# Moving steps of the opening, of the end of self attention and of the output path in a decoder layer

## The chip, the core and the metric

The kernel runs on one core of a Trainium2 chip. The metric is the device time in microseconds (us) of one execution. The engines are named as in the profile: PE is TensorE (PEld its weight loads), DVE is VectorE, ACT is ScalarE, POOL is GpSimd, SP is the sync engine that issues transfers.

## What is computed

One decoder layer over 8 batches of 512 tokens of 256 features, in float32. The reference, cut to its stages:

```python
x = layernorm(x + self_attn(x))            # 16 heads, gated linear attention with level factors and decays
x = layernorm(x + cross_attn(x, ctx_1024)) # 16 heads of 16, 1024 keys, softmax, output projection
x = layernorm(x + ffn(x))                  # 32 experts, each takes its top 8 tokens

# in self_attn
dt  = softplus(x @ Wdt.T + dt_bias); g = -exp(A_log) * dt
Lam = softplus(Lp * (x @ Wdl.T))
decay = exp(cumsum(g)[t] - cumsum(g)[s])
W = (Q K^T) * S ** -0.5 * decay * Lam[level(t, s)]
y = (W V) @ Wout.T + x
```

## The kernel before

**Order of stages.** `self_attention`, `cross_attention` and `experts_and_combine` run one after the other, each in a block of its own: the next begins when all engines have finished the one before. Every engine has its own program with waits on semaphores. In the two attentions the work goes through sections `first` (batch 0), `mid` (batches 1 to 6), `last` (batch 7) and `tail`. In a section, `now` is the batch in work, `prev` the batch before, whose last pieces are still to be done, and `nxt` the batch behind, which is being prepared.

**Opening of self attention** (`sec == "pro"`). DVE evaluates log1p as a polynomial twice: over the level factors `lam` (`log1p_poly`, nine instructions of 640 columns, L93 and L96) and over the time steps `dt_g` (nine of 512 columns). For the latter `decay_sums` first adds a bias to PE's result, writes a tile of ones and forms -|z|, and waits for ACT's exponential of it (L761). A scan gives `cg` (`cg_ready`). PE transposes `cg`, POOL forms distances from it, ACT exponentiates them, and PE and ACT turn them into `dec` (`dec_ready`). `spread_sums` hands the sums to POOL's `differences` (L856), ACT takes their absolute value and exponential (L785, L787), and DVE multiplies the result into `NEAR` (L1046). `level_factors` (L1027 to L1031) and `block_factors` (L1001, L1005) stand behind `spread_sums`.

**End of self attention** (`sec == "tail"`, i = 0 to 7, of which PE has 4). PE finishes the last two head pairs, transposes y (L465), projects it (L673), and also prepares batch 0 of cross attention: `cross_tokens` (transposes of x, L575), `cross_queries` (L585), `cross_keys` (L601) and `cross_values` (L593). `sa_jobs` and `CROSS_JOBS` list the same jobs in the same order for the PSUM slots. DVE splits queries and keys into three bf16 parts (`parts`, L186 to L195), and does the layer norm between.

**Cross attention.** A batch has 32 steps: 4 quads of heads by 8 chunks of 128 keys. In each step PE makes the scores of four heads (L1489), which ACT exponentiates (L1625), multiplies the step before by the values (L1450), and makes four tiles of scores for the maxima 12 steps ahead (L1428), which DVE reduces (L1716); these tiles have three PSUM slots, used in turn. Every eighth step PE also transposes the maxima (L1437) and DVE copies them out (L1737). The other work of a batch is tied to steps: PE transposes the next batch's x in step 0, projects half of its own values in step 1 (L1415), the next batch's queries in step `PROJECT_Q` = 4 (L1406) and its keys in steps 7 and 12 (L1398), transposes the previous batch's normalised x in step 9 (L1561), and projects the values' other half in step 20.

**Outputs.** When a quad of heads is done, `take_outputs` transposes its sum out of PSUM (L1744). `outputs` then takes a reciprocal (L1750), multiplies (L1752) and transposes again (L1756), and SP copies the result into `oT` (`move_o`, L1281). For quads 2 and 3 of the previous batch both calls stand in step 1. In step `PROJECT_O` = 4, PE waits for the copies (`o_moved`) and projects the outputs (L1507), DVE adds x and forms mean and variance (L1782 to L1791, `var`), and in step `NORM` = 7 normalises (L1795). Quad 0 of the batch in work is scaled and transposed in step `GATE_MAX` = 12, just ahead of the gate's MAX8.

**POOL in cross attention** does its work in this order, whatever the steps are; the splitting of queries and keys takes four pieces of four operations each:

```python
if prev:
    pool.wait_ge(var, b)
    nc.gpsimd.tensor_tensor(rstd[:, :, 0], mv[:, :, 1], sh.mhalf[:, 0:G], ALU.pow).then_inc(rstd_ready, 1)
if nxt:
    ...
    parts(ca, pool, nc.gpsimd, 2, b * 3 + 4, pieces=4)
```

`parts` first waits until ACT has copied the projection into the one buffer `R`; ACT in its turn (`evac_whole`) copies the next projection only when the parts of the one before have been made:

```python
src = full(name)
act.wait_ge(parts_ready, (b + 1) * 3 + (n + 1) % 3)
nc.scalar.copy(R[:], src).then_inc(act_evac, 1)
```

Scores and projections share two PSUM slots (`psA`), in the fixed order that `ca_jobs` lists, and ACT's queue is in order too.

Of the kernel before, what the change touches and what calls it, by code (L numbers as in the profile page):

```python
# [88 lines left out]

def log1p_poly(eng, acc, u):  # L90

    c = _log1p_coefficients()
    eng.tensor_scalar(acc, u, c[0], None, ALU.mult)  # L93
    eng.drain()
    for ck in c[1:]:
        eng.scalar_tensor_tensor(out=acc, in0=acc, scalar=ck, in1=u, op0=ALU.add, op1=ALU.mult)  # L96
        eng.drain()
# [39 lines left out]
STACKED = 16 * 2 * len(Q_PARTS)  # L137
X1T, PROJECT_V1, PROJECT_Q, PROJECT_O, NORM = 0, 1, 4, 4, 7
PROJECT_K, X2T, COPY_X2, GATE, GATE_MAX, GATE_EXP, TOP8, TOP8_T, PICK, PICK_T = (7, 12), 9, 10, 10, 12, 14, 20, 21, 28, 29
PROJECT_V0, LAST_OUTPUTS = 20, 27  # L140
BEHIND_JOBS = (PROJECT_V1 + 1, PROJECT_K[0] + 1)
# [133 lines left out]

CROSS_JOBS = {0: ["cq"], 2: [("ck", 0)], 3: [("ck", 1), "cv"]}


def sa_jobs(section):

    now, prev, nxt = flags(section)
    a, v = [], []
    if section == "pro":
        return ["dl", ("v", 0)], v
    for i in range(PAIRS if now else 4):
        a += [("state", i)] * (sa_pair(section, i, 2) is not None)
        a += ["x1T"] * (i == 0 and section == "tail")
        a += [("qk", i)] * now
        a += ["yT"] * (i == 2 and prev)
        a += [("ktok", i)] * (sa_pair(section, i, 1) is not None)  # L290
        a += ["dl"] * (i == 0 and nxt) + [("v", 1)] * (i == 2 and now) + [("v", 0)] * (i == 5 and nxt)
        a += CROSS_JOBS.get(i, []) if section == "tail" else []
        v += [("score", i)] * (sa_pair(section, i, 1) is not None)
        v += [("far", i)] * (sa_pair(section, i, 2) is not None)
        v += [("out", 0), ("out", 1)] * (i == 3 and prev)
    return a, v
# [4 lines left out]
SA_DVE = Lane({s: sa_jobs(s)[1] for s in SECTIONS}, DVE_SLOTS)  # L301
SCALE = S ** -0.5
ZERO = len(_log1p_coefficients())
POOL_POLY = {2: (0, 2)}
# [11 lines left out]
def self_attention(nc, sh, dram):  # L316
    with ExitStack() as ctx:
# [103 lines left out]
        def _(pe):  # L421
            def body(sec, b):
# [194 lines left out]
                for i in range(PAIRS if now else 4):  # L617
                    one, two = sa_pair(sec, i, 1), sa_pair(sec, i, 2)
                    if two is not None:
                        states(i, two)  # L620
                    if sec == "tail" and i == 0:
                        cross_tokens()
                    opening = sec == "first" and i == 1
# [52 lines left out]
                    if sec == "tail":  # L676
                        if i == 0:
                            cross_queries()
                        if i == 2:
                            pe.wait_ge(ca.ctx_loaded, 16)  # L680
                            cross_keys(0)
                        if i == 3:
                            cross_keys(1)
                            pe.wait_ge(ca.wv_loaded, 16)
                            cross_values()
# [5 lines left out]
        def _(act):  # L691
            def body(sec, b):
# [71 lines left out]
                for i in range(PAIRS):  # L764
                    steps = i < (PAIRS if now else 4)
                    if steps and sa_pair(sec, i, 2) is not None:
                        nc.scalar.copy(Mst[:, 1:16, :], full(("state", i))[:, HD:16 * HD].rearrange("q (s c) -> q s c", c=HD)
                                       ).then_inc(act_evac, 1)
                    if sec == "tail" and i == 0:
                        nc.scalar.copy(ca.x1T[:].rearrange("p k t -> p (k t)"), full("x1T")).then_inc(act_evac, 1)  # L770
                    if now:
# [28 lines left out]
                    if i == 6 and nxt:  # L800
                        decays()
                    if sec == "tail" and i == 0:
                        cross_whole("cq", 0)
                    if sec == "tail" and i == 6:
# [173 lines left out]
        def _(dve):  # L978
# [3 lines left out]
            def body(sec, b):  # L982
# [81 lines left out]

                def decay_sums():

                    dve.wait_ge(dt_full, 1)
                    nc.vector.tensor_scalar(dt_z, bank(0), dtb[:, 0:1], None, ALU.add)
                    nc.vector.memset(ones, 1.0)
                    dve.drain()  # L1070
                    negated_abs(nc, dt_g, dt_z).then_inc(dt_abs, 1)
                    dve.wait_ge(dt_exp, 1)
                    log1p_poly(nc.vector, dt_g, dt_u)

                    nc.vector.scalar_tensor_tensor(out=dt_g, in0=dt_z, scalar=0.0, in1=dt_g, op0=ALU.max, op1=ALU.add)
                    dve.wait_ge(rate_ready, 1)
                    dve.drain()
                    nc.vector.tensor_scalar(dt_g, dt_g, alog[:, 0:1], -1.0, ALU.mult, ALU.mult)
                    dve.drain()
                    nc.vector.tensor_tensor_scan(out=cg, data0=ones, data1=dt_g, initial=0.0, op0=ALU.mult, op1=ALU.add  # L1080
                                                 ).then_inc(cg_ready, 1)

                if sec == "pro":
                    nc.vector.memset(ca.zero[:], 0.0)
                    dve.wait_ge(level_loaded, 16 * 3)
                    dve.wait_ge(expz, 1)
                    log1p_poly(nc.vector, lam[:].rearrange("p g h l -> p (g h l)"), ul[:])
                    dve.wait_ge(dt_loaded, 16 * 3)
                    decay_sums()
                    dve.wait_ge(cgt_ready, 1)  # L1090
                    spread_sums()
                    level_factors()
                    block_factors()
                    dve.wait_ge(zeroed, 3)
                    dve.wait_ge(dec_ready, 1)
                    return
# [129 lines left out]
def cross_attention(nc, sh, dram):  # L1226
    with ExitStack() as ctx:
# [467 lines left out]
        def _(dve):  # L1695
# [8 lines left out]
            def body(sec, b):  # L1704
# [25 lines left out]
                def max_rows(pos):  # L1730
                    for name in max_step(pos)[1]:
# [7 lines left out]
                        dve.nop().then_inc(dve_evac, 1)  # L1739

                def take_outputs(bb, q):

                    dve.wait_ge(av_done, (bb * QUADS + q + 1) * KT)
                    nc.vector.transpose(byq[q % 2][:].rearrange("p c s -> p (c s)"), acc[:]).then_inc(acc_evac, 1)  # L1744
                    dve.drain()

                def outputs(bb, q):

# [4 lines left out]
                                            ALU.mult)  # L1753
                    dve.drain()
                    dve.wait_ge(o_moved[q % 2], bb * 32 + (q // 2 + 1) * 16)
                    nc.vector.transpose(byd[q % 2][:], t[:].rearrange("p c s -> p (c s)")).then_inc(o_ready, 1)  # L1756
# [9 lines left out]
                for s in range(STEPS if now else TAIL_STEPS):  # L1766
                    maxima = now and (nxt or s + LEAD < STEPS)
                    if maxima:
                        max_jobs(s + LEAD, 0, 1)
                    if prev and s == 1:  # L1770
                        if sec != "tail":
                            outputs(b - 1, 2)
                        outputs(b - 1, 3)
                    if prev:
# [31 lines left out]
                        if s == GATE_MAX:  # L1806
                            if sec == "mid":
                                dve.wait_ge(l_moved, b * (16 * G))
                            if now:
                                outputs(b, 0)  # L1810
                            nc.vector.max(m8[:], L[:])
# [19 lines left out]
                        if s == PICK_T:  # L1831
                            nc.vector.tensor_copy(sh.mT[:, :, :, bass.ds(b - 1, 1)].rearrange("p k e o -> p k (e o)"),
                                                  full("mT")[:, 0:KD * P].rearrange("p (k e) -> p k e", k=KD)[:, :, 0:E]
                                                  ).then_inc(dve_evac, 1)
                    if sec == "first" and s == GATE_MAX:
                        outputs(b, 0)
                    if now and s == TOP8:
# [379 lines left out]
```

## Time and profile before

| what | us |
|---|---|
| median of 3 runs (range) | 1792.65 (1788.92 to 1797.26) |
| the profiled execution, time | 1791.35 |
| its span, first to last instruction | 1789.6 |
| opening, until the steady part of self attention | 0 to 61 |
| self attention, batches | 61 to 580 |
| its end | 580 to 629 |
| cross attention, batches 0 to 7 | 661 to 1605 |
| its tail | 1605 to 1632 |
| experts and combination | 1632 to 1790 |

Busy shares over the whole span are PE 93%, DVE 71%, ACT 46% and POOL 33%. They are averages over stages with different limits; a row of the timeline tells when one instruction (or several alike, one after the other) started, how long it took, and in brackets how long its engine had been idle and what ended that.

### The profile page before, as it was taken

Reading aid. Unit: us, or ns where it says so; the run is one execution under the profiler, and the core shown is the slowest. Engines: PE = TensorE matmul, PEld = TensorE weight load, DVE = VectorE, ACT = ScalarE, POOL = GpSimd, SP = SyncE. Lnnn points to the kernel's source line nnn. Section 1 sums busy time; section 2 is a strip of 40 time slices with the busy share of each in tenths; the row PEclk is TensorE's granted clock in tenths of the full one; section 3 lists DMA queues with packets and bytes.
Section 4 is the critical chain, followed back from the end, with each engine's and each line's share of the span. In section 5 each row is a group of like instructions: output and inputs, shape, how many; then the busy total and the mean of one; then the engine's idle time right before and its main releaser. Section 6 shows DMA issues by size and latency. Waiting matters only on the chain. (4 is left out here: it accounts for less than half of the span.)

```text
span 1789.6 us, 48945 instructions
## 1 busy us (share of the span) xinstructions
PE 1659.9 (93%) x19942; PEld 802.0 (45%) x19942; DVE 1277.5 (71%) x2414; ACT 814.5 (46%) x981; POOL 587.1 (33%) x926
## 2 busy tenths in 40 slices
PE   6899999999999789999999999999999999898557
PEld 3566666666666423343343333433433434234224
DVE  5667677677774577888878889788788888842004
ACT  2334343343342215656556656565466565561103
POOL 3535545554552454316034043060250420000002
PEclk8999999999999859999999999999999999998879
DMA  7000000000000130211111202211112121438995
GB/s 258 3 4 3 3 3 3 3 3 3 3 33 3 36 93 25 86 57 44 59 57 48 92 32 78 67 44 59 57 44 81 36 74 60 192 116 344 420 419 217
DMA packets 66062, 146.04 MB, mean 82 GB/s; under 512 B 12320, under 2 KB 36128, under 8 KB 58176
## 3 DMA queue, kind: packets, MB, share of 16 engines
q1 hardware_dynamic: 65296, 142.34, 21.9%
q8 instruction: 157, 2.57, 0.6%
q10 hardware_dynamic: 560, 0.72, 0.2%
q14 instruction: 49, 0.40, 0.1%
HBM read 92.43 MB, written 7.86 MB: 56 GB/s over the span
## 5 line engine op out<-in xcount | busy, mean ns | idle before, releaser
L1716 DVE TENSOR_REDUCE mx<-cpsV 128x1 f32<-128x512 f32 x1024 | 652.9, 685 | 114.2 <-PE cpsV L1428 93.7
L1625 ACT ACTIVATE w<-cpsA 128x1024 f32<-128x1024 f32 x512 | 496.3, 1021 | 253.6 <-PE cpsA L1489 248.5
L1428 PE MATMUL cpsV<-w 96*128 96x512 bf16 x1024 | 332.5, 394 | 29.0 <-DVE mx L1716 16.1
L1489 PE MATMUL cpsA<-w 99*128 99x512 bf16 x1024 | 272.3, 381 | 5.8 <-ACT w L1603 3.4
L1450 PE MATMUL cacc<-w 128*32 128x512 f32 x2048 | 273.3, 606 | 0.4 <-ACT w L1625 0.4
L472 PE MATMUL psA<-w 128*128 128x512 f32 x512 | 257.9, 627 | 8.3 <-DVE WT L1105 3.5
L1428 PEld LDWEIGHTS cpsV<-w 96*128 96x128 bf16 x1024 | 85.3, 98 | 308.8 <-DVE mx L1716 227.5
L1683 POOL TENSOR_TENSOR crstd<-cmv,mhalf 128x4 f32<-128x4 f32 x8 | 8.2, 1019 | 579.9 <-DVE cmv L1791 579.9
L772 ACT COPY w<-psA 128x1024 f32<-128x1024 f32 x64 | 64.8, 1013 | 233.4 <-PE psA L472 233.4
L1489 PEld LDWEIGHTS cpsA<-w 99*128 99x128 bf16 x1024 | 93.8, 97 | 135.3 <-ACT w L1625 10.9
L890 POOL TENSOR_TENSOR VP<-V,VPF 128x128 f32<-128x128 f32 (+2 forms) x256 | 130.1, 540 | 44.4 <-PE psA L485 39.8
L1114 DVE TENSOR_TENSOR tmp<-psV,CF 128x512 f32<-128x512 f32 x64 | 44.3, 692 | 112.4 <-PE psV L535 111.9
L472 PEld LDWEIGHTS psA<-w 128*128 128x128 f32 x512 | 88.4, 192 | 79.8 <-issue 69.3
L186 POOL TENSOR_TENSOR w<-w,zero 128x256 bf16<-128x256 f32 x88 | 51.2, 613 | 122.1 <-ACTq L1604 122.1
L1450 PEld LDWEIGHTS cacc<-w 128*32 128x32 f32 x2048 | 41.0, 108 | 94.0 <-issue 89.8
L2114 DVE TENSOR_TENSOR z<-psE,b1T 128x256 f32<-128x256 f32 x8 | 3.4, 425 | 110.7 <-PE psE L2044 110.7
L2058 PE MATMUL psE<-w,hT 128*32 128x256 f32 x512 | 37.6, 458 | 38.7 <-DMA w<-in_w 36.8
L1121 DVE TENSOR_REDUCE w<-tmp 128x128 f32<-128x512 f32 x64 | 67.6, 1056 | 4.7
L1603 ACT COPY w<-cpsA 128x1024 f32<-128x1024 f32 x21 | 21.3, 1013 | 96.5 <-PE cpsA L1398 49.7
L505 PEld LDWEIGHTS psV<-w 64*32 64x32 f32 x4096 | 41.2, 106 | 48.9 <-issue 47.7
L1415 PEld LDWEIGHTS cpsA<-w,w 128*128 128x128 f32 x480 | 54.7, 192 | 12.6 <-ACT w L1625 12.6
L195 POOL TENSOR_TENSOR w<-w 128x256 bf16<-128x256 f32 x88 | 57.2, 679 | 3.1
(232 smaller groups left out, 2202.3 us busy)
## 6 DMA issues: line engine op xcount, KB each, us to landing
w<-in_w SPq DMA_DIRECT2D x56, 1024.0 KB, 16.4
w<-w SPq DMA_DIRECT2D x189, 128.0 KB, 2.3
w<-w SPq DMA_DIRECT2D x189, 64.0 KB, 2.0
w<-in_ctxT SPq DMA_DIRECT2D x8, 1024.0 KB, 5.2
w<-in_xT SPq DMA_DIRECT2D x8, 512.0 KB, 6.4
x_tok<-in_x SPq DMA_DIRECT2D x8, 512.0 KB, 9.7
w<-in_w SPq DMA_DIRECT2D x8, 512.0 KB, 17.2
out_y<-w SPq DMA_DIRECT2D x16, 256.0 KB, 2.3
```

The costliest lines, as they stand in the source:

```text
L186: ops.tensor_tensor(cut(high, m), cut(r, m), zeros, ALU.add)
L195: ops.tensor_tensor(cut(low, m), cut(r, m), cut(mid, m), ALU.subtract)
L472: last = nc.tensor.matmul(out[:, n * T:(n + 1) * T], w[:, k, i * P:(i + 1) * P], XT[:, b, k, :], start=(k == 0), stop=(k == KD - 1))
L772: nc.scalar.copy(QK[:, i % 4, :], full(("qk", i))).then_inc(act_evac, 1)
L890: last = nc.gpsimd.tensor_tensor(VP[:, p % 2, g, 0:n, :].rearrange("q n (h c) -> q n h c", c=HD), vv.unsqueeze(1).broadcast_to([P, n, 2, HD]),
L1121: nc.vector.tensor_reduce(yp, tmp[:].rearrange("p g s c -> p g c s"), AX_X, ALU.add)
L1415: last = nc.tensor.matmul(out[:, c * P:(c + 1) * P], cT[:, k, c * P:(c + 1) * P], wv[:, k, hv * P:(hv + 1) * P], start=(k == 0), stop=(k = ...
L1428: nc.tensor.matmul(out, Qst[q // 2][0:ROWS, hh, g * P:(g + 1) * P], Kst[q // 2][0:ROWS, hh, half * BANK:(half + 1) * BANK], start=True, st ...
L1450: last = nc.tensor.matmul(acc[BLK * jj:BLK * (jj + 1), :], Vc[:, chunk, 4 * q + jj, :], Pr[:, (2 * s + jj // 2) % 4, (jj % 2) * T:(jj % 2 ...
L1489: last = nc.tensor.matmul(out[:, n * T:(n + 1) * T], Kst[q // 2][0:ROWS + 3, hh, chunk * P:(chunk + 1) * P], Qst[q // 2][0:ROWS + 3, hh, : ...
L1625: nc.scalar.activation(Pr[:, (2 * s + pp) % 4, :], src, ACT.Exp, scale=CA_SCALE).then_inc(act_evac, 1)
L1716: nc.vector.tensor_reduce(mx[:, q % 2, row, k % 2:k % 2 + 1], full(m[k]), AX_X, ALU.max).then_inc(dve_evac, 1)
```

## The change

Four things are moved; no arithmetic is added or dropped.

1. Opening: seven of the nine polynomial instructions over `lam` come first, then bias, ones and -|z| of the time steps, then the last two, then `level_factors`, then the polynomial over the time steps and the scan. `level_factors` stood behind `spread_sums`.
2. End of self attention: the transposes of x stand at the end of i = 0 and no longer near its start, the queries in i = 1 and not 0, the first half of the keys in i = 3, behind the output projection, and not in i = 2.
3. Cross attention, quad 0: reciprocal and multiplication are in step 9, the transposition stays in step 12.
4. Cross attention, quad 3 of the previous batch: `outputs` stands in step 4 and not 1 (but in `tail` in step 1, as before), and the output projection with its additions and statistics in step 5 and not 4.

```diff
-def log1p_poly(eng, acc, u):
+def log1p_poly(eng, acc, u, first=0, last=None):
...
-X1T, PROJECT_V1, PROJECT_Q, PROJECT_O, NORM = 0, 1, 4, 4, 7
+X1T, PROJECT_V1, PROJECT_Q, PROJECT_O, NORM = 0, 1, 4, 5, 7
...
-PROJECT_V0, LAST_OUTPUTS = 20, 27
+PROJECT_V0, LAST_OUTPUTS, SCALE_OUTPUTS = 20, 27, 9
...
-CROSS_JOBS = {0: ["cq"], 2: [("ck", 0)], 3: [("ck", 1), "cv"]}
+CROSS_JOBS = {0: ["x1T"], 1: ["cq"], 3: [("ck", 0), ("ck", 1), "cv"]}
...
-                    if sec == "tail" and i == 0:
-                        cross_tokens()
...
                     if sec == "tail":
                         if i == 0:
+                            cross_tokens()
+                        if i == 1:
                             cross_queries()
-                        if i == 2:
+                        if i == 3:
                             pe.wait_ge(ca.ctx_loaded, 16)
                             cross_keys(0)
-                        if i == 3:
                             cross_keys(1)
...
-                    log1p_poly(nc.vector, lam[:].rearrange("p g h l -> p (g h l)"), ul[:])
+                    lamf = lam[:].rearrange("p g h l -> p (g h l)")
+                    log1p_poly(nc.vector, lamf, ul[:], 0, BEFORE_STEPS)
                     dve.wait_ge(dt_loaded, 16 * 3)
+                    time_steps()
+                    log1p_poly(nc.vector, lamf, ul[:], BEFORE_STEPS)
+                    level_factors()
                     decay_sums()
                     dve.wait_ge(cgt_ready, 1)
                     spread_sums()
-                    level_factors()
                     block_factors()
...
-                    if prev and s == 1:
-                        if sec != "tail":
-                            outputs(b - 1, 2)
+                    if prev and s == 1 and sec != "tail":
+                        outputs(b - 1, 2)
+                    if prev and s == (1 if sec == "tail" else PROJECT_O - 1):
                         outputs(b - 1, 3)
...
                             if now:
-                                outputs(b, 0)
+                                turn_outputs(b, 0)
...
+                    if now and s == SCALE_OUTPUTS:
+                        scale_outputs(b, 0)
                     if sec == "first" and s == GATE_MAX:
-                        outputs(b, 0)
+                        turn_outputs(b, 0)
```

`scale_outputs` is the first half of `outputs` (reciprocal and multiplication, each with a drain), `turn_outputs` the second (the wait for the buffer and the transposition); `time_steps` is the first part of `decay_sums` up to -|z|.

## Rows read from the trace of the kernel before

**Rows 1.** windows, batch 2: length, busy PE PEld DVE ACT POOL, clock, DMA share
```profile
894.67:1015.70 121.03, 118.41 (x670) 45.37 (x669) 102.89 (x195) 69.79 (x75) 35.61 (x57) 1.00 0.18 59
```

**Rows 2.** timeline, TensorE, batch 2: start, length, line, operands, count
```profile
912.60 3.69 PE L1507 MATMUL cpsV<-cwo,oT 128*128 128x256 f32 x16
...
917.22 3.70 PE L1406 MATMUL cpsA<-w 128*128 128x512 f32 x8
...
923.07 1.07 PE L1450 MATMUL cacc<-w 128*32 128x512 f32 x8
...
924.51 0.81 PE L1489 MATMUL cpsA<-w 99*128 99x512 bf16 x3
...
929.73 3.70 PE L1398 MATMUL cpsA<-w,w 128*128 128x512 f32 x8
```

**Rows 3.** timeline, VectorE, batch 2, steps 1 and 4; idle before in brackets
```profile
903.36 0.26 DVE L1750 RECIPROCAL rec<-byq 128x16 f32<-128x16 f32 x1
...
904.19 0.71 DVE L1756 STREAM_TRANSPOSE byd<-byq 128x512 f32<-128x512 f32 x1
...
914.72 0.69 DVE L1782 TENSOR_TENSOR o<-cpsV,x_tok 128x512 f32<-128x512 f32 x1
...
918.51 0.17 DVE L1791 TENSOR_SCALAR cmv<-cmv 128x4 f32<-128x4 f32 x1
```

**Rows 4.** timeline, GpSimd, batch 2, steps 4 to 7
```profile
918.76 1.03 POOL L1683 TENSOR_TENSOR crstd<-cmv,mhalf 128x4 f32<-128x4 f32 x1 [69.66 <-DVE cmv L1791]
...
922.16 2.33 POOL L186 TENSOR_TENSOR w<-w,zero 128x256 bf16<-128x256 f32 x4 [2.37 <-ACTq L1604]
...
929.80 2.70 POOL L195 TENSOR_TENSOR w<-w 128x256 bf16<-128x256 f32 x4
```

**Rows 5.** timeline, ScalarE, batch 2, step 7
```profile
933.54 1.01 ACT L1603 COPY w<-cpsA 128x1024 f32<-128x1024 f32 x1 [3.55 <-PE cpsA L1398]
```

**Rows 6.** source view of L1281, the copies of outputs
```profile
DMA to landing us min/median/max: 2.6/2.6/6.3
```

**Rows 7.** timeline, batch 2, steps 9 and 13
```profile
940.63 2.62 DVE L1716 TENSOR_REDUCE mx<-cpsV 128x1 f32<-128x512 f32 x4 [0.93 <-PE cpsV L1428]
...
954.75 0.10 PEld L1428 LDWEIGHTS cpsV<-w 96*128 96x128 bf16 x1 [0.60 <-DVE mx L1716]
```

**Rows 8.** timeline, TensorE, batch 7, steps 4 and 13
```profile
1516.00 3.69 PE L1507 MATMUL cpsV<-cwo,oT 128*128 128x256 f32 x16
...
1553.52 0.39 PE L1428 MATMUL cpsV<-w 96*128 96x512 bf16 x1 [2.69 <-DVE mx L1716]
```

**Rows 9.** windows around gaps of TensorE; columns as in group 1
```profile
44.80:47.30 2.50, 0.00 (x0) 0.00 (x0) 2.27 (x7) 2.50 (x3) 2.36 (x9) 1.00 0.01 3
...
50.70:54.20 3.50, 0.04 (x3) 0.01 (x1) 3.28 (x5) 0.65 (x2) 1.82 (x2) 0.80 0.00 0
...
54.20:59.60 5.40, 5.40 (x47) 2.82 (x48) 1.67 (x8) 1.01 (x1) 3.63 (x3) 0.50 0.01 2
...
1554.70:1558.10 3.40, 3.40 (x13) 0.73 (x6) 2.28 (x4) 0.04 (x1) 0.00 (x0) 0.50 0.12 42
```

**Rows 10.** timeline, end of self attention
```profile
603.18 4.88 PE L601 MATMUL psA<-w,w 128*128 128x512 f32 x8
...
607.90 3.62 PE L673 MATMUL psV<-wo,w 128*128 128x256 f32 x16
...
618.58 1.23 DVE L195 TENSOR_TENSOR w<-w 128x1024 bf16<-128x1024 f32 x1
```

**Rows 11.** timeline, opening
```profile
25.03 0.43 DVE L93 TENSOR_SCALAR w<-w 128x512 f32<-128x512 f32 x1 [0.69 <-ACT w L761]
...
47.76 1.91 ACT L787 ACTIVATE w<-w 128x2048 f32<-128x2048 f32 x1
...
51.05 1.27 DVE L1046 TENSOR_TENSOR w<-w,w 128x1024 f32<-128x1024 f32 x1
```

**Rows 12.** source view of L1031: count, ns min/median/max, first and last start
```profile
L1031 DVE TENSOR_SCALAR w<-w,tconst x40: 266/274/1087, 40.7 to 510.3; 128x64 f32<-128x64 f32 x40
```

More of the change, by code:

```diff
@@ L87, in negated_abs @@
     return nc.vector.scalar_tensor_tensor(out=out, in0=x, scalar=-1.0, in1=x, op0=ALU.mult, op1=ALU.min)
-def log1p_poly(eng, acc, u):
+def log1p_poly(eng, acc, u, first=0, last=None):
     c = _log1p_coefficients()
-    eng.tensor_scalar(acc, u, c[0], None, ALU.mult)
-    eng.drain()
-    for ck in c[1:]:
+    if first == 0:
+        eng.tensor_scalar(acc, u, c[0], None, ALU.mult)
+        eng.drain()
+    for ck in c[max(first, 1):last]:
         eng.scalar_tensor_tensor(out=acc, in0=acc, scalar=ck, in1=u, op0=ALU.add, op1=ALU.mult)
@@ L286, in sa_jobs @@
         a += [("state", i)] * (sa_pair(section, i, 2) is not None)
-        a += ["x1T"] * (i == 0 and section == "tail")
         a += [("qk", i)] * now
@@ L302 @@
 SCALE = S ** -0.5
+BEFORE_STEPS = 7
 ZERO = len(_log1p_coefficients())
@@ L768, in body @@
                                        ).then_inc(act_evac, 1)
-                    if sec == "tail" and i == 0:
-                        nc.scalar.copy(ca.x1T[:].rearrange("p k t -> p (k t)"), full("x1T")).then_inc(act_evac, 1)
                     if now:
@@ L802, in body @@
                     if sec == "tail" and i == 0:
+                        nc.scalar.copy(ca.x1T[:].rearrange("p k t -> p (k t)"), full("x1T")).then_inc(act_evac, 1)
+                    if sec == "tail" and i == 1:
                         cross_whole("cq", 0)
@@ L1063, in output_factors, with time_steps @@
                     dve.drain().then_inc(lam_used, 1)
-                def decay_sums():
+                def time_steps():
                     dve.wait_ge(dt_full, 1)
@@ L1071, in decay_sums @@
                     negated_abs(nc, dt_g, dt_z).then_inc(dt_abs, 1)
+                def decay_sums():
                     dve.wait_ge(dt_exp, 1)
@@ L1739, in max_rows, with outputs @@
                         dve.nop().then_inc(dve_evac, 1)
+                def outputs(bb, q):
+                    scale_outputs(bb, q)
+                    turn_outputs(bb, q)
                 def take_outputs(bb, q):
@@ L1745, in take_outputs, with scale_outputs @@
                     dve.drain()
-                def outputs(bb, q):
+                def scale_outputs(bb, q):
                     t = byq[q % 2]
@@ L1754, in outputs, with turn_outputs @@
                     dve.drain()
+                def turn_outputs(bb, q):
+                    t = byq[q % 2]
                     dve.wait_ge(o_moved[q % 2], bb * 32 + (q // 2 + 1) * 16)
```

## Prediction

> **What bounds the kernel now.** I read the page, then the busy times by windows, then the timeline stage by stage. In the windows the reader is to see that a batch of cross attention takes 121.03 us, of which PE is busy 118.41, at full granted clock [rows 1]. There are six such batches (1 to 6), each within 0.9 us of this length. So PE is the bound, DVE (102.89) stands close behind, and POOL (35.61) seems far off. That last share misleads: in the timeline POOL's work lies in bursts that ACT, and through ACT PE, must wait for. What is moved is therefore judged by order and due time, not by busy time.
>
> In the timeline of batch 2 the steps 4 to 8 read so: PE projects the outputs from 912.60 to 916.29, then the queries from 917.22 to 920.92, begins step 6 at 924.51 and the first half of the keys at 929.73 [rows 2]. DVE gives the variance at 918.68 [rows 3], POOL has its power done at 919.79, then idles 2.37 us until ACT has copied the queries, and splits them from 922.16 to 932.50: 10.34 us [rows 4]. ACT copies the keys at 933.54, and by its row it waited for PE's projection [rows 5]. POOL's split was done only 1.04 us before. That margin is what the change spends.
>
> **Output projection in step 5 (batches 1 to 6).** Steps 4 and 5 first. The projection's 3.69 us leave step 4 and enter step 5; the queries come 3.66 earlier. DVE now scales quad 3 where it began the additions, at 914.72; from the reciprocal to the end of the transposition that takes 903.36 to 904.90 = 1.54 [rows 3], so the copy is issued at about 916.35 and lands 2.6 us later [rows 6], near 919.0. Everything of step 5 up to its values, which stood at 923.07 [rows 2], comes 3.66 earlier too (the queries used to follow at once on the projection, 917.22 against 913.56 now), and the projection takes the place of the values: 923.07 − 3.66 = 919.4. The copy is in time by 0.4 us, the projection ends at E = 923.1, and step 6 begins 1.4 later (923.07 to 924.51 is 1.44 [rows 2]), where it began before. The step's PE work is neutral. Bounds: 0, and 3.7 if the copy takes its longest, 6.3.
>
> Now what hangs on it. From the projection's end (916.29) to the variance (918.68) are 2.39 us, to the end of the power 3.50 [rows 3, 4]. The query projection used to lie in those 3.5 us, so POOL waited for ACT. Now ACT has copied the queries at 922.1 − 3.7 = 918.4, but POOL, in order, waits for `var`: it starts the split at E + 3.6 and ends at E + 3.6 + 10.34 = E + 13.95 = 937.05. ACT can have PE's keys at E + 1.4 + (933.54 − 924.51) = E + 10.4 = 933.5; about 0.5 of DVE's statistics also come between PE and its next tile in step 6, which this wait swallows. ACT may copy only when the split is done, so it stands 3.5 us, with the exponentials of step 8 behind it; PE makes two scores and two tiles and stands too, since the next scores need the slot that ACT has not emptied. DVE has nothing to reduce. I find nothing that hides it: 3.5 us in each of six batches = **+21.0**. The next projection (step 12) comes 19 us later, and POOL's second split takes 10.2: no further wait. SP's later copy also holds back the context's transfer, which the queue has behind it: from 905.7 to about 917; with a median landing of 5 us it is there by 922, needed at 930. The maxima's copy behind that is needed in step 8 too. Both nothing.
>
> **Clock.** PE would stand from about 935.3 (two tiles after step 8's first scores) to 938.1, 2.8 us. After a gap of 3.5 us the clock was granted at 0.50 for the next 5.4 us; after the gap of 2.69 in batch 7 it was 0.50 for 3.40 us; after one of 2.5 us it stayed at 1.00 in that stretch [rows 8, 9]. In a low stretch of 3.40 us PE does what takes 1.7 at the full level. I take 1.7 in five of the six batches: **+8.5**; bounds 0 (no drop) and 6 × 3.4 = 20.4 (a stretch of 6.8). The Trainium skill (TensorE: Matmul & The Clock Gate, "HAM oscillation — how this bites in real kernels") says that a wait which returns in each tile can put the clock down each time, half of the low time being lost; by it the term would be 6 × 1.7 = 10.2 and the forecast 1.7 higher. The row at 44.8 is why I count five.
>
> **Quad 0 scaled in step 9.** Reciprocal and multiplication are 0.83 us (903.36 to 904.19 [rows 3]). In step 9 DVE idles 0.93 us while PE transposes x [rows 7]: covered, in batches 1 to 7. What they leave is step 12, whose overrun PE meets in step 13: a wait of 0.60 at 954.75 [rows 7] and one of 0.5 behind it, of which step 13's excess over batch 0 is 0.65. I take 0.65 × 6 = **−3.9**, bounds 0 and 6 × 0.83. In batch 7 PE waits 2.69 there [rows 8] with nothing to cover: −0.8. Batch 0 has no transposition of x in step 9: +0.3.
>
> **Batch 7.** It projects no queries, so step 4 has only 2.83 us of PE work against DVE's maxima, row factors and now the scaling. DVE's copy is ready 3.75 after where the projection began (912.60 to 916.35), so at 1516.00 + 3.75 + 2.6 + 0.1 = 1522.45 landed; PE could project one step later than before, at 1518.85 [rows 8]. The wait is 3.6, of which 0.5 is now spent on DVE anyway: **+3.1**, with step 13 +2.3. Bounds 0 and 3.6. The tail keeps its scaling in step 1 and has no steps' work between; nothing changes. Weights for the experts follow the end of this stage, so a shift here reaches the end.
>
> **End of self attention.** Before, the keys' half (4.88 us from 603.18) stood ahead of the output projection at 607.90, and everything behind ran through DVE: additions, statistics and the split of the keys until 619.81 [rows 10], then ACT for another 8.8. Now y is done ahead of the queries. PE's sum from the last head pair is queries (3.6 to 5.4, by clock) + transposes 1.4 + ACT's copy 1.1, now uncovered, + projection 3.62 + keys 3.6 to 4.88, which with 1.0 for ACT's copy and 5.1 for the split puts the split's end at 614.4 to 617.9. Against 619.81: −5.4 to −1.9; I take **−3.8**.
>
> **Opening.** ACT's exponential, for which DVE idled 0.69 [rows 11], is now behind two polynomial instructions. `level_factors` comes in ahead of `cg`: its five L1031 take 0.27 each when POOL is quiet and up to 1.09 beside POOL [rows 12]; with the two others 2.2 us. `cg` comes 1.5 later, and all of POOL, ACT and PE that follows it. DVE has 5 us less behind it, but `NEAR` at 51.05 waits for ACT's exponential, done at 49.67 [rows 11], which moves by the same 1.5; only DVE's last doubling between (1.4) falls away. Net **+0.2**, bounds 0 and +1.5.
>
> **Sum.** 21.0 + 8.5 − 3.9 + 0.3 + 2.3 − 3.8 + 0.2 = +24.6. On the profiled execution's 1791.35 us that is 1816. The median of the runs is 1.3 above the profiled time; I leave that inside the range.
>
> **Rivals.**
> - *The wait, but the clock holds* (chance 0.20). For it: the row at 44.8, and PE works until 2.8 us before the copy. Then 1791.35 + 16.1 = 1807.5.
> - *Longer low stretches* (0.12): 6.8 us each, as seen from 52.8 to 59.6 in the opening; 1791.35 + 16.1 + 20.4 = 1828.
> - *The split of the queries ends in time* (0.06), the other side. It decides at 10.4 − 3.6 = 6.8 us for the split, or if `var` came 3.5 us earlier. Against it: all its operations of 2.3 to 2.7 us for four are steady rows. Then only −3.9, +0.3, +2.3, −3.8, +0.2 stay: 1786.5, not slower.
> - *Nothing shows* (0.04): each gain and loss is eaten by slack elsewhere, 1791 to 1796.
>
> My forecast has 0.58. Range: the forecast's own runs from 1809 to 1823 by the ends of the self-attention and batch 7 terms; to hold 8 in 10 it must take in the first rival, and with the copy's late landings part of the second: 1802 to 1829. A change under 0.5% (9 us) can hardly be told from none here: faster 0.03, same 0.09, slower 0.88.
>
> **What would show it.** Step by step in the profile after: in batches 1 to 6 ACT's copy of the keys (L1603, step 7) ended by POOL, some 3.5 us after PE's projection, and the same batches near 125 to 126 us instead of 121.0; the granted clock below 1.00 in them; no wait of PE for DVE in step 13; DVE idle in step 1; the first cross-attention instruction about 4 us earlier than 628.9; batch 7 about 2 us longer. It is wrong if the copy L1603 still follows PE directly, for then the largest term is gone, or if PE waits for `oT` in step 5 by more than 0.5 us.

## The result and the profile after

| | before | after |
|---|---|---|
| median of the runs (range), us | 1792.65 (1788.92 to 1797.26) | 1824.69 (1819.52 to 1826.51) |
| profiled execution: time, span | 1791.35, 1789.6 | 1819.52, 1817.8 |

The changed kernel is slower: the ratio is 1.0168, with a 95% interval of 1.0139 to 1.0196. The profiled execution is the shortest of the three of after; the other two took 5.2 and 7.0 us more, at a mean granted clock of 0.954 and 0.953 against 0.959. Of the 28.2 us between the two profiled spans, the part up to cross attention's first reduction gives back 8.0, batch 0 takes 1.6, batches 1 to 6 take 27.8, batch 7 takes 6.1 and the stages behind it 0.7.

The windows of after, one for each batch shown (columns as in [rows 1]), then one low stretch of the clock in batch 1:

```profile
768.06:893.74 125.68, 121.04 (x670) 46.55 (x669) 102.73 (x195) 69.79 (x74) 35.74 (x57) 0.97 0.17 57
893.74:1018.71 124.97, 119.68 (x670) 45.74 (x669) 103.01 (x195) 69.79 (x74) 35.73 (x57) 0.99 0.17 57
...
1144.92:1272.65 127.73, 122.47 (x670) 46.50 (x669) 102.60 (x195) 69.89 (x75) 35.70 (x57) 0.96 0.17 56
...
1397.83:1521.32 123.49, 118.14 (x669) 45.34 (x668) 102.76 (x195) 69.79 (x75) 30.62 (x49) 1.00 0.18 58
1521.32:1627.30 105.98, 98.93 (x531) 33.05 (x529) 72.36 (x145) 63.85 (x69) 1.02 (x1) 0.94 0.35 138
811.90:818.70 6.80, 6.80 (x26) 2.54 (x23) 3.88 (x7) 2.78 (x4) 6.38 (x11) 0.50 0.00 0
```

Two losses are to be seen. Batch 6 ran at full granted clock and with no more busy time of PE than [rows 1], and still took 123.49 (120.88 before): this is waiting. The others took 1.5 to 4.2 us more than batch 6, the more the lower their mean clock: 0.99, 0.97, 0.96.

The wait stands in the timeline of after, batch 1, steps 4 to 8, rows of all engines in order of time:

```profile
786.14 3.70 PE L1412 MATMUL cpsA<-w 128*128 128x512 f32 x8
...
788.10 0.71 DVE L1771 STREAM_TRANSPOSE byd<-byq 128x512 f32<-128x512 f32 x1
...
788.84 0.51 SPq L1287 DMA_DIRECT2D oT<-byd  x1
...
789.96 1.01 ACT L1609 COPY w<-cpsA 128x1024 f32<-128x1024 f32 x1 [3.56 <-PE cpsA L1412]
...
791.91 3.62 PE L1513 MATMUL cpsV<-cwo,oT 128*128 128x256 f32 x16
...
797.73 0.17 DVE L1806 TENSOR_SCALAR cmv<-cmv 128x4 f32<-128x4 f32 x1
...
797.98 1.02 POOL L1689 TENSOR_TENSOR crstd<-cmv,mhalf 128x4 f32<-128x4 f32 x1 [73.57 <-DVE cmv L1806]
...
798.97 2.33 POOL L187 TENSOR_TENSOR w<-w,zero 128x256 bf16<-128x256 f32 x4
...
802.74 3.70 PE L1404 MATMUL cpsA<-w,w 128*128 128x512 f32 x8
...
806.76 2.55 POOL L196 TENSOR_TENSOR w<-w 128x256 bf16<-128x256 f32 x4
...
809.39 1.01 ACT L1609 COPY w<-cpsA 128x1024 f32<-128x1024 f32 x1 [6.39 <-POOLq L197]
...
810.46 0.61 PE L1495 MATMUL cpsA<-w 99*128 99x512 bf16 x2 [2.63 <-ACT w L1609]
```

ACT had copied the queries at 790.97, but POOL split them only from 798.97, because it stood at the power (L1689), which needs the variance of 797.90. In [rows 4] the order was the same, but the power was over before the queries had been copied. The split ends at 809.31; ACT's copy of the keys, in [rows 5] released by PE, is now released by POOL, and PE waits 2.63 us for the slot that ACT has not emptied. The page's costliest groups say it for the whole kernel (busy, mean ns, idle before, and how much of it the named releaser ended):

```profile
L1495 PE MATMUL cpsA<-w 99*128 99x512 bf16 x1024 | 278.0, 387 | 21.3 <-ACT w L1609 19.1
...
L1609 ACT COPY w<-cpsA 128x1024 f32<-128x1024 f32 x21 | 21.3, 1012 | 91.6 <-POOLq L197 38.3
```

38.3 is six times 6.39, one wait in each of the batches 1 to 6. The 6.80 us at granted clock 0.50 begin 1.4 us after PE's wait has ended, with PE at work in between.

The timeline of TensorE after, in the opening, the end of self attention, batch 7, and the end of the kernel:

```profile
54.22 1.98 PE L473 MATMUL psA<-w 128*128 128x512 f32 x4 [1.71 <-DVE WT L1111]
...
592.01 3.70 PE L586 MATMUL psA<-w 128*128 128x512 f32 x8
...
598.03 3.69 PE L672 MATMUL psV<-wo,w 128*128 128x256 f32 x16 [1.45 <-ACT w L772]
...
1541.83 0.39 PE L1434 MATMUL cpsV<-w 96*128 96x512 bf16 x1 [1.06 <-DVE mx L1722]
...
1543.66 6.42 PE L1513 MATMUL cpsV<-cwo,oT 128*128 128x256 f32 x16 [0.64 <-DMA oT<-byd]
...
1803.15 1.99 PE L2016 MATMUL psE<-x_tok,ident 128*128 128x256 f32 x8 [3.11 <-ACT w L2119]
```

### The profile page after: what moved, and what is told of

Read it like the earlier page. It is cut to its first block and busy times, and to the rows that moved or that the text cites. A ratio compares the mean times of both kernels' runs of the same rounds, so it can differ in the third digit from the quotient of the medians.

```text
span 1817.8 us, 48945 instructions
## 1 busy us (share of the span) xinstructions
PE 1667.3 (92%) x19942; PEld 802.7 (44%) x19942; DVE 1275.6 (70%) x2414; ACT 814.7 (45%) x981; POOL 586.8 (32%) x926
## 5 line engine op out<-in xcount | busy, mean ns | idle before, releaser
L1434 PE MATMUL cpsV<-w 96*128 96x512 bf16 x1024 | 337.0, 399 | 28.7 <-DVE mx L1722 18.5
L1495 PE MATMUL cpsA<-w 99*128 99x512 bf16 x1024 | 278.0, 387 | 21.3 <-ACT w L1609 19.1
L1456 PE MATMUL cacc<-w 128*32 128x512 f32 x2048 | 277.9, 615 | 0.4 <-ACT w L1631 0.4
L1689 POOL TENSOR_TENSOR crstd<-cmv,mhalf 128x4 f32<-128x4 f32 x8 | 8.1, 1018 | 622.0 <-DVE cmv L1806 622.0
L1495 PEld LDWEIGHTS cpsA<-w 99*128 99x128 bf16 x1024 | 95.0, 99 | 155.3 <-ACT w L1609 27.8
L187 POOL TENSOR_TENSOR w<-w,zero 128x256 bf16<-128x256 f32 x88 | 51.2, 614 | 114.6 <-ACTq L1610 114.6
L1609 ACT COPY w<-cpsA 128x1024 f32<-128x1024 f32 x21 | 21.3, 1012 | 91.6 <-POOLq L197 38.3
L1421 PEld LDWEIGHTS cpsA<-w,w 128*128 128x128 f32 x480 | 54.7, 192 | 12.6 <-ACT w L1631 12.6
```

Of the source, the lines that this page charges most:

```text
L1421: last = nc.tensor.matmul(out[:, c * P:(c + 1) * P], cT[:, k, c * P:(c + 1) * P], wv[:, k, hv * P:(hv + 1) * P], start=(k == 0), stop=(k = ...
L1434: nc.tensor.matmul(out, Qst[q // 2][0:ROWS, hh, g * P:(g + 1) * P], Kst[q // 2][0:ROWS, hh, half * BANK:(half + 1) * BANK], start=True, st ...
L1456: last = nc.tensor.matmul(acc[BLK * jj:BLK * (jj + 1), :], Vc[:, chunk, 4 * q + jj, :], Pr[:, (2 * s + jj // 2) % 4, (jj % 2) * T:(jj % 2 ...
L1495: last = nc.tensor.matmul(out[:, n * T:(n + 1) * T], Kst[q // 2][0:ROWS + 3, hh, chunk * P:(chunk + 1) * P], Qst[q // 2][0:ROWS + 3, hh, : ...
```

## The experiments

Each ratio is to the kernel before in the same session (medians 1790.7 to 1791.8), with its 95% interval. Lengths of batches are those of the one profiled execution, measured from the first exponential of one batch to that of the next, batch 7's to its last step.

**Part 4 undone, parts 1 to 3 kept.**

```diff
-X1T, PROJECT_V1, PROJECT_Q, PROJECT_O, NORM = 0, 1, 4, 5, 7
+X1T, PROJECT_V1, PROJECT_Q, PROJECT_O, NORM = 0, 1, 4, 4, 7
-                    if prev and s == 1 and sec != "tail":
-                        outputs(b - 1, 2)
-                    if prev and s == (1 if sec == "tail" else PROJECT_O - 1):
-                        outputs(b - 1, 3)
+                    if prev and s == 1:
+                        if sec != "tail":
+                            outputs(b - 1, 2)
+                        outputs(b - 1, 3)
```

> The changed kernel with quad 3's scaling back in step 1 and the output projection back in step 4; opening, end of self attention and the scaling of quad 0 stay changed. Theory (the order of GpSimd's queue: the variance comes late, so the split of the queries ends late, so ScalarE's copy of the keys and with it TensorE waits in step 8): batches 1 to 6 return to about 120.3 us (121.0 less 0.7 for step 13), batch 7 to about 99, the whole about 1780, that is 40 below the changed kernel and 11 below the kernel before. Rival (what stands in steps 9 and 12, or the opening, costs something in the batches): batches 1 to 6 stay above 121.

Measured: 1784.13 us, ratio 0.9957 (0.9944 to 0.9971). Batches 1 to 6 have full clock and 120.2 to 120.4 us each but for the first (119.54). The window of batch 2:

```profile
886.70:1007.08 120.38, 118.06 (x670) 45.39 (x669) 103.08 (x195) 69.81 (x74) 35.75 (x57) 1.00 0.18 59
```

Against the 121.03 of [rows 1] that is 0.65 us less, all of it in step 13 (2.93 us for 3.59): the quad scaled in step 9. Everything that made the change slow is in part 4. The batches came out as expected, the whole 4 us above the 1780 that was expected.

**Part 4 kept, GpSimd's order turned round.** The query split now stands ahead of the wait for the variance.

```diff
-                if prev:
-                    pool.wait_ge(var, b)
-                    nc.gpsimd.tensor_tensor(rstd[:, :, 0], mv[:, :, 1], sh.mhalf[:, 0:G], ALU.pow).then_inc(rstd_ready, 1)
                 if nxt:
...
                     parts(ca, pool, nc.gpsimd, 2, b * 3 + 4, pieces=4)
+                if prev:
+                    pool.wait_ge(var, b)
+                    nc.gpsimd.tensor_tensor(rstd[:, :, 0], mv[:, :, 1], sh.mhalf[:, 0:G], ALU.pow).then_inc(rstd_ready, 1)
```

> The changed kernel, and in GpSimd's queue the split of the queries is put ahead of the wait for the variance; output projection stays in step 5. Theory (GpSimd's order): no wait of TensorE for ScalarE's copy in step 8, no low clock there, batches 1 to 6 at about 120.8 us (123.5 in batch 6 of the changed kernel less 2.8), the whole about 31 below the changed kernel, near 1789. Rival (the projection in step 5 has lost the cover that the query projection gave, and that by itself is the loss): batches stay near 124, at most 1 us less each.

Measured: 1790.95 us, ratio 1.0005 (0.9992 to 1.0017). The timeline of its batch 2, then the windows of batches 2 and 7:

```profile
910.35 1.01 ACT L1609 COPY w<-cpsA 128x1024 f32<-128x1024 f32 x1 [3.55 <-PE cpsA L1412]
...
911.48 2.32 POOL L187 TENSOR_TENSOR w<-w,zero 128x256 bf16<-128x256 f32 x4 [68.78 <-ACTq L1610]
...
921.84 1.03 POOL L1693 TENSOR_TENSOR crstd<-cmv,mhalf 128x4 f32<-128x4 f32 x1 [0.18 <-issue]
...
927.03 1.01 ACT L1609 COPY w<-cpsA 128x1024 f32<-128x1024 f32 x1 [3.55 <-PE cpsA L1404]
```

```profile
887.64:1008.52 120.88, 118.04 (x670) 45.43 (x669) 101.57 (x195) 69.79 (x75) 35.59 (x57) 1.00 0.18 59
1491.78:1598.11 106.33, 99.25 (x531) 32.52 (x529) 72.41 (x145) 63.84 (x68) 1.02 (x1) 0.94 0.35 138
```

POOL splits at once, the keys' copy is released by PE again, and both the waits and the low clock are gone from batches 1 to 6. So not the moved projection as such, but the order of two things in POOL's queue made each of the six batches 4.8 us longer (753.3 us for the six in after, 724.2 here). What is left of the moved steps is 0.5 us a batch: 120.7 to 120.9 for the 120.2 to 120.4 with part 4 undone. Batch 7 stays at 106.

**Part 4 alone, on the kernel before** (the first diff, the other way round).

> The kernel before with the fourth part alone: quad 3 scaled in step 4, projection in step 5. Theory: all of the loss is in this part, so this is the slowest kernel: batches 1 to 6 at 124.2 us without a low clock and 125 to 129 with, batch 7 longer by 6, in sum 1791 + 19 + 12 + 6 = about 1828, some 9 above the changed kernel. Rival (the parts act together, the other three are neutral): about 1820, as the changed kernel.

Measured: 1820.39 us, ratio 1.0158 (1.0140 to 1.0176). Batches 1 to 6 took 123.4, 125.78, 127.14, 125.83, 125.58 and 124.09, the first and the last of them at full clock:

```profile
1402.25:1526.34 124.09, 118.48 (x669) 45.29 (x668) 102.56 (x195) 69.81 (x74) 30.40 (x49) 1.00 0.17 57
```

124.09 − 120.88 = 3.2 us of wait without the scaling's gain, near the predicted 3.5. The expected 1828 was missed; the time is the rival's 1820, and the other three parts gain nothing here that the runs can tell (after has 1.0168). In the two traces they do gain, 7.1 us ahead of batch 0 and 0.65 in each batch, but the clock takes much of it back: the low stretches of batches 1 to 6 add up to 30.6 us in after and to 17.1 in this trace.

**The wait filled.** In batches 1 to 6, ahead of step 8's first scores, PE makes 20 transposes of the identity into the slot that the scores then overwrite.

```diff
                             out = take_a(("s", s, pp))
+                            if s == 8 and pp == 0 and sec == "mid":
+                                for _ in range(20):
+                                    nc.tensor.transpose(out[:, 0:P], sh.ident[:], sh.ident[:])
```

> The changed kernel with 20 transposes of the identity (about 2.3 us of TensorE, results overwritten) ahead of the first scores of step 8 in batches 1 to 6, where TensorE would stand for 2.6 us anyway. Theory (part of the loss is the clock, which falls after the wait): the wait stays, the clock stays at full level, batches 1 to 6 all near 123.6 us, in sum 12 below the changed kernel's profiled 1819.5, about 1808. Rival (the low clock is hidden behind ScalarE and VectorE): as the changed kernel, or slower by the added work.

Measured: 1810.84 us, ratio 1.0102 (1.0082 to 1.0122), 0.66% or 12 us under the ratio of after, although nothing useful was added. The window of its batch 2, and in TensorE's timeline the fill and the wait that is left:

```profile
895.27:1018.91 123.64, 120.30 (x690) 47.65 (x689) 102.97 (x195) 69.81 (x75) 35.75 (x57) 1.00 0.18 58
```

```profile
934.77 2.35 PE L1495 MATMUL cpsA<-ident 128*128 128x128 f32 x20
936.96 0.60 PE L1498 MATMUL cpsA<-w 99*128 99x512 bf16 x2
...
938.54 0.61 PE L1498 MATMUL cpsA<-w 99*128 99x512 bf16 x2 [0.55 <-ACT w L1612]
```

ACT's copy still waits for POOL (6.41 us in this run), the batches take 123.4 to 123.6 (the first 122.77), like batch 6 of after, and no clock below 1.00 is granted in any of them. The six sum to 740.5 against 753.3 in after: 12.8 us for the clock. Against the 721.1 of part 4 undone the wait is the rest: 19.4 us, 3.2 a batch.

**The projection in step 5 in batch 7 alone, on the kernel before.** Quad 3 is turned in step 4 and the outputs projected in step 5 only where `sec == "last"`.

```diff
+def project_o(sec):
+    return 5 if sec == "last" else PROJECT_O
...
-                        outputs(b - 1, 3)
+                        if sec != "last":
+                            outputs(b - 1, 3)
+                    if sec == "last" and s == 4:
+                        outputs(b - 1, 3)
```

> The kernel before with one edit: in the last section alone, quad 3 of batch 6 is turned in step 4 and the output projection stands in step 5. The prediction priced this at 3.1 us (a wait of PE for the copied outputs). Theory by the trace of after: steps 4 and 5 together take 15.5 us where they took 10.4, a wait of about 3.5 with the clock then low, so batch 7 gets 4 to 6 us longer (99.8 before) and the time is 1794.5 to 1797. Rival one (the prediction's price, no clock): 3 us, 1793.5 to 1794.5. Rival two (slack later in the section takes it up): no change, 1790 to 1792.

Measured: 1797.46 us, ratio 1.0028 (1.0012 to 1.0045); some 5 us. TensorE's timeline of its batch 7:

```profile
1517.35 0.39 PE L1433 MATMUL cpsV<-w 96*128 96x512 bf16 x1 [1.06 <-DVE mx L1721]
...
1519.18 6.45 PE L1512 MATMUL cpsV<-cwo,oT 128*128 128x256 f32 x16 [0.62 <-DMA oT<-byd]
...
1556.02 1.21 PE L1433 MATMUL cpsV<-w 96*128 96x512 bf16 x2 [2.70 <-DVE mx L1721]
```

The projection took 6.45 where it took 3.69 [rows 8], 2.76 by the clock. Steps 4 to 6 are 5.6 us longer than in before: PE stood 2.8 us in them for 0.7, and was busy 16.1 for 12.6, in a low stretch of 6.8 us from 1517.9 on. Of the standing only 0.62 is for the copied outputs; the larger part is for DVE's maxima, behind the moved scaling and transposition. Steps 13 and 14 took another 2.6 in this execution, with a low stretch from 1555.5, within the wait of 2.70, to 1565.7; that wait is as long in before [rows 8]. Rival two (no change) falls by the interval. Rival one (a wait of 3 us and no clock) doesn't, since 3 us lie within it, but it falls by the trace, where the clock is low.

**Batch 7 put back, GpSimd's order turned, on the kernel after.** The second diff, and the projection in step 4 where `sec == "last"`.

> The kernel after with two edits: GpSimd splits the queries ahead of its wait for the variance, and in the last section alone quad 3 of the batch before is turned in step 1 and the output projection stands in step 4, as in the kernel before. The run with the first edit alone took 1790.95 us, and its batch 7 lasted 106.3 us to step 31, against 98.9 where the whole output path was put back. Theory (batch 7 has no query projection to cover the later copy, so the moved step costs it 5 to 7 us): batches 1 to 6 stay at 120.7 to 121.0, batch 7 lasts 99 to 102, and the time is 1784 to 1787. Rival (batch 7's excess was a low stretch of the clock that fell there by chance): batch 7 stays at 104 to 107 or lengthens elsewhere by the same, and the time is 1790 to 1792.

Measured: 1787.79 us, ratio 0.9974 (0.9957 to 0.9990). Batch 7:

```profile
1495.40:1594.08 98.68, 93.90 (x531) 30.81 (x529) 72.53 (x145) 63.85 (x68) 1.02 (x1) 0.98 0.38 148
```

98.68 for 106.33; the time is 0.8 above the theory's bound. The rival is half right: 4.6 of these 7.7 us lie in steps 4 to 6, which the edit puts back, and 3.1 in steps 13 and 14, where this execution had 3.4 us of low clock and the other 10.2. Even without the wait and without batch 7 the step brings nothing over leaving it undone: batches 1 to 6 took 120.8 to 121.2 but for the first, 0.5 to 0.8 more than with part 4 undone. Where these go is not shown.

**The opening alone, and the end of self attention alone, each on the kernel before** (parts 1 and 2 of the change).

> The kernel before with the new opening alone. The changed kernel reached the second head pair at the same time as before (54.2 us) but was 2.3 us ahead from 60 us on. Theory (TensorE waits 1.7 us there and no longer 3.5, so its clock does not fall and what follows runs in half the time): 2.3 to 2.6 us less than before, granted clock 1.00 from 54 to 60. Rival (the gain belongs to another part, or the run's own clock state): 0, clock 0.50 there.

> The kernel before with the new order at the end of self attention alone. Theory (the output projection no longer stands behind half of the keys, and the split of the keys follows it): the last block of self attention ends 5.4 us earlier; forecast of the prediction 3.8, between 1.9 and 5.4. Rival (the gain came from the opening's shift of the clock's phase): 2 us or less, with a low clock in 590 to 606 as in the kernel before.

Measured: 1791.17 us, ratio 0.9990 (0.9973 to 1.0008), and 1790.95 us, ratio 0.9990 (0.9972 to 1.0008). Neither moves the whole time by an amount that the runs can tell; the intervals reach from 5 us less to 1.4 more. In the first, the clock still fell after PE's wait in the opening, as the rival had it, and the first reduction of cross attention came at 629.3, where it was (629.8). TensorE's timeline, then that of part 4 undone, which has the same opening:

```profile
54.91 3.32 PE L474 MATMUL psA<-w 128*128 128x512 f32 x4 [2.07 <-DVE WT L1113]
```

```profile
49.45 3.39 PE L473 MATMUL psA<-w 128*128 128x512 f32 x4
...
53.83 1.98 PE L473 MATMUL psA<-w 128*128 128x512 f32 x4 [0.24 <-DVE WT L1111]
```

One trace doesn't settle it. With the new opening and nothing filled in there, the four matmuls behind the wait took 1.98 us in five of seven traces; in four of these five a low stretch of 3.4 us fell ahead of the wait, as in the second fence, and cost nothing there. With the old opening they took 3.48 to 3.78 in all four.

In the second run the first reduction came at 623.6, 6.2 us earlier, with no low clock from 590 to 606, as the theory had it; but batch 7 had a low stretch from 1547.4 to 1557.6 and took 102.5 (99.8 before), and the stages behind it took 2.7 more. Part of these 6.2 us is the clock's and not the order's. From one and the same copy of ACT near 555 us to the first reduction, the old order took 73.6 to 73.8 us with 6.8 us of low clock in two stretches, 72.4 with 6.8 in one, and 70.1 with 3.4; the new order took 69.9 to 70.2 with 6.8 and 66.2 to 68.3 with none. At equal low time the order is worth 2.2 to 3.9 us.

**The opening's wait filled, on the kernel before.**

```diff
+                    if sec == "first" and i == 2:
+                        for _ in range(24):
+                            nc.tensor.transpose(qk[:, T:T + P], sh.ident[:], sh.ident[:])
                     if two is not None:
```

> The kernel before with 24 transposes of the identity on TensorE in the opening, where it waits 3.5 us for VectorE at 50.7 us; their results are overwritten. Nothing else is moved. Theory (the gain of the opening is the clock's): the clock stays at full level from 54 to 60 and self attention's batches begin 2 us earlier, though VectorE's work is as before. Rival (the gain comes from VectorE's shorter chain): no gain, or a small loss.

Measured: 1786.68 us, ratio 0.9970 (0.9953 to 0.9988). In TensorE's timeline the four matmuls that took 1.98 in after do so here too:

```profile
54.04 1.98 PE L472 MATMUL psA<-w 128*128 128x512 f32 x4 [0.70 <-DVE WT L1108]
```

They start when they did, but at full clock: the gain that the new opening has in after can be had without any of its reordering. By the first reduction of cross attention this execution is 6.4 us ahead of before. Of these 3.7 lie at the end of self attention, where nothing was changed: between 580 and 610 us one low stretch fell there and not two.

**Two versions meant to be best.** The first is part 4 undone, with batch 0 alone scaled in step 12 as before; the second is part 4 undone with the 24 transposes.

> The changed kernel with the output path of quad 3 and the projection back in steps 1 and 4, and quad 0 scaled in step 9 only where a batch before is being finished (batch 0 scales in step 12 again). By the parts: opening -2.3, end of self attention -5.4, step 13 of six batches -4.1, batch 7 -0.8 to -2.5: 1791.4 - 13.5 = about 1778, and 0.7 below the run with the outputs put back. Rival (the clock's low stretch at the start of cross attention falls into batch 0 and takes some back): 1780.

> The kernel after with part 4 of the change undone (which alone took 1784.13 us) and 24 transposes of the identity into PSUM that nobody reads, in the opening, where PE waits for the first distances (which alone, on the kernel before, gave 1786.68, 4 us less than before). Theory (both work on the clock at 52 to 60 us, where the new opening has already removed part of the low stretch): together 1781 to 1784, with the first reduction of cross attention at 618 to 621 us. Rival (they are independent and add up): 1780 or less, at 617 or earlier. If the clock only moves its low stretches elsewhere: 1784 to 1786.

Measured: 1784.13 us, ratio 0.9957 (0.9934 to 0.9979), and 1779.65 us, ratio 0.9942 (0.9922 to 0.9962). Batch 0 went back from 114.6 to 113.0 in the first, 0.8 of it the scaling, with no effect on the whole that the runs can tell; the expected 1778, and the rival's 1780, were missed. The second has the lowest median, as its rival had it (1780 or less), but the intervals overlap, and its mechanism isn't shown: the 24 transposes ran past the result that PE waits for (they end at 55.2, the matmuls behind them started at 54.2 in after), the first reduction came at 620.5 (621.0 with part 4 undone), where the theory had it and not at the rival's 617, and what this execution gained lies in batch 7, which for once has full clock:

```profile
1487.78:1585.16 97.38, 92.40 (x531) 30.69 (x529) 72.55 (x145) 63.84 (x69) 1.02 (x1) 1.00 0.39 150
```

Both versions are faster than the kernel before, and so than the changed one.

## Why the prediction was right

Predicted were 1816 us and a range of 1802 to 1829; 1824.69 came out, the profiled execution at 1819.52. The mechanism, its place and the sign were as forecast; that the sum came so near is partly luck, since its errors cancel. The sizes, in the order of the sum:

- **Wait for the split, +21.0.** Right, and a little too large: 19.4 between part 4 undone and the filled wait. From E, the projection's end at 795.53, the variance came 2.4 later, and the split ended at E + 13.8 (predicted 13.95). By the steps of batch 6, step 7 grew by 2.83 and step 6 by 0.62, together 3.45 for the predicted 3.5; of this the growth in step 6 is where the 0.5 of DVE's statistics was expected. Steps 4 and 5 together shrank by 0.19 (predicted neutral), and PE did not wait for `oT` there. Shown by turning POOL's order alone.
- **Clock, +8.5.** Too small: the filled wait puts it at 12.8. The count of five batches of six came out, by luck: with part 4 alone, and the same wait of 2.6 us in each batch, it was four. Their low stretches were 6.8, 3.4, 6.8, 10.2 and 3.4 us, not 3.4 each. The bound of 20.4 held. By the Trainium skill (TensorE: Matmul & The Clock Gate, "HAM oscillation — how this bites in real kernels") a wait that returns in each tile puts the clock down each time, and half of the low time is lost. Here the clock fell in five of six batches, and half of their 30.6 us would be 15.3, while 12.8 was measured; that the rest fell into time in which PE would have waited anyway is a guess.
- **Quad 0 in step 9, −3.9.** Right: 0.65 us per batch (120.38 for 121.03) with part 4 undone. Batch 0 lost more than the 0.3: 1.6 us, of which 0.8 lie in step 10, behind the scaling, and the rest in steps 0 and 1, which begin at low clock: it lasts 4.9 us into batch 0, and 2.4 in before.
- **Batch 7, +3.1 and −0.8.** Mis-sized: +6.1 in after. Steps 4 to 6 grew by 5.6, in after and when done alone, and the parts are others than predicted. The projection began where the prediction put it, 7.1 us after the first exponential of step 4 for 7.2. But PE stood 2.8 us in these steps for 0.7 before, so the wait is 2.1 and not 3.1, and only 0.64 us of it is for `oT`; most of it is for DVE's maxima, which now come behind the scaling and the transposition. PE was busy 16.0 us for 12.6: 3.5 us for the clock, already low when the projection began, which took 6.42 for 3.69. I had priced it for the six batches and not for the seventh. The −0.8 is there as a wait: ahead of step 13's tiles PE stood 1.86 or 1.87 us in every trace with the scaling in step 9, and 2.69 or 2.70 in every one without. But low stretches of 0 to 10.2 us begin at this wait, from one execution to the next, and hide it: in after step 13 is 0.4 shorter and step 14 1.0 longer.
- **End of self attention, −3.8.** At the bound: −5.4. The queries (592.01) took 3.70 where the estimate's upper end had 5.4, because the clock stayed up, and the wait for ACT's copy was 1.45 for the 1.1 assumed. At equal low time the order is worth 2.2 to 3.9 us, by the traces above; the rest of the 5.4 is the clock's.
- **Opening, +0.2.** The path of the data was priced rightly: the scan starts 1.2 us later (34.24 for 33.00), the doubling at `NEAR` starts where it did (51.01 for 51.05), and PE is released at 54.22 for 54.19. The step that failed is that an equal release means an equal time. PE now waited 1.71 us there and not 3.46, the clock stayed up, and the next four matmuls took 1.98 and not 3.78: −2.5. The opening alone, in another execution, had a low stretch behind the wait again. So the −2.5 comes through the clock. The new opening had it in five of seven traces and the old one in none of four; that it moves the low stretch reliably is not shown.

The errors partly cancel. Against the predicted sum of 24.6 the profiled execution lost 28.2 − 24.6 = 3.6 more: the clock in the six batches +3.7 (12.2, when the 2.6 by which batch 6 grew is taken for the wait in all six), batch 7 +3.8, batch 0 +1.3 and the stages behind +0.7 on one side; opening and end −4.4, and the six batches' 15.6 of wait less scaling for the predicted 17.1, −1.5, on the other.

## What to carry to other kernels

When a step moves in one engine's program, write down for each in-order queue what is due before it and after it: here the 3.5 us from the projection to the end of the power, harmless at its place before, came to lie ahead of a 10 us job on the engine with the lowest busy share, and an exchange of two statements there took 4.8 us a batch away again. Price every new or removed wait of TensorE twice, once as time and once as clock, and in every section of the loop. And before crediting a reordering with a gain of a few us, fill the wait with work that nobody reads: where that gives the same, the gain was the clock. One trace isn't enough for such a gain either; compare all traces that have the same order at that place.

## What the runs showed of the chip

**The same wait does not always cost the same clock.** Batches 1 to 6 of after all have a TensorE wait of about 2.6 us ahead of step 8, and the low stretches behind it lasted 6.8, 3.4, 6.8, 10.2, 3.4 and 0 us. Near the kernel's end PE waits 3.11 to 3.13 us for ACT in all thirteen traces. In five of them, before and after among these, the clock stays at 1.00 for at least 8 us behind the wait, and the transposes there take 1.99 or 2.00 (shown above). In eight it is at 0.50 within 1.5 us of the wait's end. One of them is the version with batch 0 scaled in step 12, whose timeline of TensorE follows; the transposes took 3.78, twice:

```profile
1764.57 3.78 PE L2016 MATMUL psE<-x_tok,ident 128*128 128x256 f32 x8 [3.12 <-ACT w L2119]
...
1770.28 3.78 PE L2016 MATMUL psE<-x_tok,ident 128*128 128x256 f32 x8
```

From the end of the wait to the start of the last products it took 9.4 us here and 4.9 in after. Such differences of 3 to 5 us are as large as the gains at the front of the kernel. By the ratios the opening alone and the end alone give 1.8 us each and the scaling 0.65 in each of six batches, in sum 7.5, and part 4 undone, which has all three, 7.7; each of these three ratios is uncertain by 2 to 3 us, so whether the parts add up can't be told. That the low stretches shift from one execution to the next with the start of the work is an inference from these profiles; no run controlled it.

**The clock also fell behind short waits.** In batch 7 of after it was granted at 0.50 from 1542.4. In the 6 us before PE had waited 0.26, 0.30 and 1.06 us, and no longer. And a wait of the same length, at the same place, with the same work before it goes either way. TensorE in batch 7, step 13, with part 4 undone, and then with part 4 undone and the 24 transposes in the opening, 1,480 us earlier:

```profile
1541.04 0.39 PE L1434 MATMUL cpsV<-w 96*128 96x512 bf16 x1 [1.86 <-DVE mx L1722]
...
1542.17 1.93 PE L1456 MATMUL cacc<-w 128*32 128x512 f32 x8
```

```profile
1540.52 0.39 PE L1437 MATMUL cpsV<-w 96*128 96x512 bf16 x1 [1.86 <-DVE mx L1725]
...
1541.44 1.06 PE L1459 MATMUL cacc<-w 128*32 128x512 f32 x8
```

The products behind the wait took 1.93 us in the one and 1.06 in the other.
